# The reciprocal of the attention sums on VectorE alone, in place of two ScalarE steps and a Newton step

## The reference, cut to what matters

```python
x = x + attention(conditioning1(x, fside, fside, w1, u1, cond))      # 16 heads of 32, causal
x = x + ffn(conditioning2(x, fside, fside, w2, u2, cond))            # 512 -> 2048 -> 512, rounded to small floats

# conditioning: a forward and a backward scan over the tokens
ek, ekv = exp(min(k, 30)), exp(min(k, 30)) * v
nf, df = scan(a * decay + ekv), scan(b * decay + ek)                 # and the same in reverse
num, den = nf + nb - ekv + euk * v, df + db - ek + euk
out = sigmoid(r) * num / max(den, 1e-8) * (0.8 + 0.2 * tf)

# attention
scores = where(causal, q @ k.T / sqrt(32), -inf)
probs = softmax(scores)                                              # exp(s - max) / sum
attn = probs @ v
return attn @ w_o.T
```

## Time and profile before

| | us |
|---|---|
| median of 3 runs | 918.21 |
| lowest and highest of them | 915.83, 919.13 |
| the profiled execution, its time | 914.99 |
| the profiled execution, its span | 913.2 |
| mean granted TensorE clock | 0.934 |

### The profile page before, as it was taken

One profiled execution on the slowest core, in us unless ns is written; L12 is line 12 of the kernel. 1 busy time (PEld: TensorE's weight loads), 2 busy tenths in 40 slices (PEclk: granted clock), 3 DMA queues, 4 the chain that ended last, 5 costly groups with the idle time before them and its releaser, 6 DMA issues.

```text
span 913.2 us, 10845 instructions
## 1 busy us (share of the span) xinstructions
PE 759.0 (83%) x3985; PEld 391.3 (43%) x3985; DVE 772.7 (85%) x1122; ACT 471.0 (52%) x710; POOL 73.8 (8%) x149
## 2 busy tenths in 40 slices
PE   4666649298889899897998999978989998999595
PEld 1222224144444344454543444544434445554483
DVE  4999999999997879889988799799887896543887
ACT  4965655358575361476653623766545325453350
POOL 1000001011100002111000021110000120200000
PEclk9676769699999999999899999999999999999798
DMA  9622211256300003754000037540000084500001
GB/s 337 256 76 90 104 57 47 57 126 163 81 23 13 1 12 93 196 150 116 13 24 1 11 73 216 151 104 24 17 7 13 15 207 113 128 1 1 1 1 46
DMA packets 30820, 72.27 MB, mean 79 GB/s; under 512 B 5808, under 2 KB 6832, under 8 KB 28976
## 3 DMA queue, kind: packets, MB, share of 16 engines
q1 hardware_dynamic: 19584, 46.67, 17.1%
q0 software_dynamic: 6144, 16.79, 7.8%
q10 hardware_dynamic: 5040, 8.14, 2.7%
HBM read 33.82 MB, written 4.19 MB: 42 GB/s over the span
## 4 chain that ended last, share of the span: by engine, by line
PE 42%; DVE 34%; issue 8%; ACT 6%; DMA 6%; SPq 3%; POOL 1%; ACTq 0%; DVEq 0%
PE bank L1499 9%; DMA stacks<-rows 5%; PE bank L1394 5%; PE bank L1306 5%; PE bank L1511 5%; PE bank L1365 3%; PE bank L1383 3%; DVE negmax L1029 3%; SPq L318 3%; PE bank L1410 2%; PE bank L1367 2%; PE bank L1332 2%; ACT region L530 2%; DVE fn L909 2%; PE bank L1298 2%
## 5 line engine op out<-in xcount | busy, mean ns | idle before, releaser
L1029 DVE TENSOR_REDUCE negmax<-bank 128x4 f32<-128x512 f32 (+2 forms) x96 | 98.7, 1035 | 39.1 <-PE bank L1339 20.6
L1365 PE MATMUL bank<-stacks 128*128 128x512 f32 (+3 forms) x256 | 106.0, 420 | 28.9 <-ACT region L530 21.0
L530 ACT ACTIVATE region<-bank 128x384 f32<-128x384 f32 (+1 forms) x192 | 95.7, 524 | 63.1 <-PE bank L1368 60.4
L318 POOL DMA_DIRECT2D stacks<-rows x128 | 69.8, 553 | 721.0 <-DVE region L806 350.2
L1306 PE MATMUL bank<-h,wqkv 128*128 128x512 f32 x256 | 115.2, 601 | 4.2 <-DVE region L1259 4.2
L1332 PE MATMUL bank<-stacks 128*128 128x128 f32 (+3 forms) x256 | 79.8, 406 | 7.2 <-DMA stacks<-rows 4.8
L1367 PE MATMUL bank<-maxrow,pick 128*128 128x512 bf16 (+3 forms) x256 | 82.9, 324 | 0.0
L1365 PEld LDWEIGHTS bank<-stacks 128*128 128x128 f32 x256 | 51.8, 202 | 59.0 <-ACT region L530 38.5
L1306 PEld LDWEIGHTS bank<-h,wqkv 128*128 128x128 f32 x256 | 48.4, 193 | 61.5 <-issue 55.4
L1298 PE MATMUL bank<-wqkv,h 128*128 128x512 f32 x128 | 60.9, 620 | 4.7 <-DVE h L957 4.7
L1552 PE MATMUL bank<-region,ident 128*128 128x512 f32 x64 | 49.0, 926 | 11.9 <-DVE identb L860 11.9
(11 more groups left out here) (178 smaller groups left out, 1485.6 us busy)
## 6 DMA issues: line engine op xcount, KB each, us to landing
stacks<-rows SPq DMA_DIRECT2D x128, 128.0 KB, 4.1
stacks<-rows POOLq DMA_DIRECT2D x128, 128.0 KB, 4.7
kt<-in_fside ACTq DMA_DIRECT2D x30, 256.0 KB, 3.3
region<-in_w_gate SPq DMA_DIRECT2D x4, 1024.0 KB, 11.3
h<-in_x SPq DMA_DIRECT2D x4, 1024.0 KB, 5.6
xt<-in_x SPq DMA_DIRECT2D x4, 1024.0 KB, 7.8
region<-in_w_up SPq DMA_DIRECT2D x4, 1024.0 KB, 6.2
region<-in_w_down SPq DMA_DIRECT2D x4, 1024.0 KB, 4.7
```

The lines of the kernel that those rows point to most:

```text
L318: eng.dma_start(stacks[HD * r:HD * r + HD, at:at + 2, i, :].bitcast(F32), rows[mine, q:k + 1:k - q, :]).then_inc(stacked[s][i], 16)
L530: nc.scalar.activation(probs[:, i, P_AT[tiles[0]]:P_AT[tiles[0]] + columns], bank[4 + n % 2][:, 0:columns], ACT.Exp, scale=SCALE).then_inc ...
L1029: nc.vector.tensor_reduce(o, scored, AX_X, ALU.max, negate=True).then_inc(max_taken, 1)
L1365: nc.tensor.matmul(o, ks[s][:, i, P * t:P * t + P], qs[s][:, i, P * t:T], start=True, stop=False, skip_group_check=True)
```

## The change

The two ScalarE steps and their semaphore go. VectorE waits for `pv_ready` itself, takes the reciprocal of bank 7 with its own instruction and multiplies bank 6 with it. Both versions have 16 divisions, four to a turn; the place of each on VectorE stays as it was, and no other instruction changes places.

```diff
-        newton, divided, rsum_ready, refined = sem("newton"), sem("divided"), sem("rsum_ready"), sem("refined")
+        newton, divided, refined = sem("newton"), sem("divided"), sem("refined")
...
-            def sum_reciprocal(b, g):
-                act.wait_ge(pv_ready, b * GROUPS + g + 1)
-                nc.scalar.activation(rsum[:, :], bank[7][:, :], ACT.Ln).then_inc(rsum_ready, 1)
-                act.wait_ge(rsum_ready, b * (2 * GROUPS) + 2 * g + 1)
-                nc.scalar.activation(rsum[:, :], rsum[:, :], ACT.Exp, scale=-1.0).then_inc(rsum_ready, 1)
-
...
-                sum_reciprocal(b, 0)
...
-                sum_reciprocal(b, 1)
...
-                sum_reciprocal(b, 2)
...
-                sum_reciprocal(b, 3)
...
             def normalise(b, g):
 
                 G = b * GROUPS + g
-                dve.wait_ge(rsum_ready, b * (2 * GROUPS) + 2 * g + 2)
-                nc.vector.tensor_tensor(attn[g], bank[7][:, :], rsum[:, :], ALU.mult).then_inc(refined, 1)
-                dve.wait_ge(refined, 2 * G + 1)
-                nc.vector.scalar_tensor_tensor(rsum[:, :], attn[g], 2.0, rsum[:, :], ALU.subtract, ALU.mult).then_inc(refined, 1)
-                dve.wait_ge(refined, 2 * G + 2)
-                nc.vector.scalar_tensor_tensor(attn[g], bank[6][:, :], -1.0, rsum[:, :], ALU.mult, ALU.mult).then_inc(normed, 1)
+                dve.wait_ge(pv_ready, G + 1)
+                nc.vector.reciprocal(rsum[:, :], bank[7][:, :]).then_inc(refined, 1)
+                dve.wait_ge(refined, G + 1)
+                nc.vector.tensor_tensor(attn[g], bank[6][:, :], rsum[:, :], ALU.mult).then_inc(normed, 1)
```

## The result

The changed kernel takes 933.41 us, median of 4 runs (932.64 to 934.9), against 917.42 for the kernel before, median of 4 (915.83 to 919.13). The ratio is 1.0176, with a 95% interval of 1.0152 to 1.020: 16.1 us slower, 13.9 to 18.3. The profiled execution took 932.64 us.

What follows compares the result with a forecast made beforehand. VectorE was taken to bound the stretch from 221 to 261 us. Turns 0 to 2 at 3.8 + 1.5 = 5.3 us each make 16.0, turn 3 adds 0: +16 on the 918.21 median, 934 us, range 922 to 950.

Steps and rivals of the forecast that it cites:

- What bounds the kernel: Turns 0 to 2, 221 to 261 us in batch 0: VectorE is busy 39.32 of 40 us and has no room.
- The size of R: Duration of VectorE's reciprocal over 512 columns, taken as 3.3 us, with 1.3 and 3.9 kept as ends.
- the reading from the long steps: Reciprocal's duration with a fixed part of 149 ns, leaving 29 ns for four columns, 7.3 a column: 3.9 us.
- Groups 0 and 1: Their divisions in turns 0 to 2: nothing absorbs 2 x 1.9 us, so group 3's transposed maxima come 3.8 us later.
- Group 2 hidden: Group 2's division, turns 0 to 2: 1.9 us more on VectorE fits in the 3.05 or 2.5 us of room.
- ScalarE's relief: TensorE's wait for group 3's exponentials goes with ScalarE's two steps in group 2: about 0.5 us a turn.
- Groups 2 and 3: Up to the second residual sum, turns 0 to 2: TensorE 1.3 us late, VectorE 1.5; the larger counts, 1.5 a turn.
- Turn 3: Batch 3, where VectorE has room: maxima may hold TensorE's scores about 0.5 us, group 2 gives 0.5 back; sum 0.
- The profile after: VectorE's busy time grows by 31 us; TensorE shows a new wait of about 1.3 us for `rows` in turns 0 to 2.

Runs made afterwards that it cites:

- the run on groups 0 and 1: Only the divisions of groups 0 and 1 in turns 0 to 2 use VectorE's reciprocal, against the kernel before: 930.34 us, ratio 1.0141.
- the runs with one of the two groups: Two kernels: only group 2, or only group 3, in turns 0 to 2 uses VectorE's reciprocal, against the kernel before: 916.32 and 916.90 us.

## Why the prediction was right

The forecast was 934.0 us, and +16; measured were 933.41 and +16.1. By its own steps:

- **What bounds the kernel.** The stretch on VectorE in turns 0 to 2, from 221 to 261 us, absorbs nothing. Shown by the run on groups 0 and 1 (+12.9; 3.77 us in each turn of the trace) and, with the sign turned, by the stretch without the Newton step (-2.8, -2.1 and -2.6 us).
- **The size of R.** 3.3 us was taken, 3.35 measured. I took a fixed part of 159 ns and divided the other 19 by three steps between four columns, which gives 6.3 ns a step and 3.4 us, and took a little less. The measured line is the same: 153 ns + 6.25 a column is 159 ns + 6.25 for each step from the first column to the last, and the durations can't tell the two forms apart. That I had the fixed part to within a ns was luck. Each ns of it moves R by 0.17 us, and the 159 came from a slip: the neighbour at 161 less its own three steps at 1.04 ns is 158, which gives 3.6, and less its four columns it is 157, which with four columns gives 2.8. In the reading from the long steps (149 ns fixed, four columns, 3.9 us) the 4 ns that the fixed part is too small are worth 0.5 us at 512 columns. One row of four columns could not decide between 2.6 and 3.9, and the range said so.
- **Groups 0 and 1**, forecast 3.8 us a turn. In batch 0 the transposed maxima of group 3 are 3.8 late. The timed run gives 4.3 a turn, with 3.5 to 5.0, and the traces 3.76 in each turn.
- **Group 2 hidden, ScalarE's relief.** The values of group 3 start at 275.97, 54.59 us after VectorE's row at 221.38, against 51.16 before: 3.4 later, 3.8 less 0.34 of relief. The forecast for the relief was 0.5; in turn 3 it is 0.50.
- **Groups 2 and 3**, forecast 1.5 us a turn, as the larger of TensorE's lateness (1.3) and VectorE's (1.5). TensorE waited 1.44 us in batch 0, VectorE's waits of 0.82, 0.57 and 0.87 are gone, the timed run gives 4.5 for three turns, and the traces 1.38 in each. VectorE's lateness is the one that counts: in turn 1 TensorE waited only 0.43 us, since it came to the projection 1.0 us later, and the stretch was as long as in the others (27.24). That it is the excess over the waits, and not a price per division, is shown by the runs with one of the two groups, whose traces have no added time.
- **Turn 3**, forecast 0: timed 1.000. The two sides that the forecast weighed, 0.5 us for the maxima of group 3 and 0.5 back from ScalarE, are both in the traces, as 0.6 later and 0.5 back.
- **The profile after.** VectorE's busy time grew by 30.2 us, forecast 31. The waits of L1382 for `rows` in turns 0 to 2 are 1.44, 0.43 and 1.44 us, forecast 1.3 each.

The duration in this trace is 3.35 us, and 6.25 ns a column is six times the 1.04 of an ordinary column. The rule of the Trainium skill that spoke against the change (the page "VectorE: DVE Perf Modes", "First, the fixed hardware budget": an iterated divide with a repeat count of 8), read as eight cycles a column, would have given an estimate of 4.4 us and +31. It pointed the right way; in size the measurement decides, and it doesn't agree.

In the profiled executions alone the difference is 17.65 us, a little more than in the medians. The two stretches of turns 0 to 2 make 15.4 of it, the change's own work. 1.7 is the feed-forward part of turn 1, at a lower granted clock; the rest is small differences of both signs outside the two stretches.

## What to carry to other kernels

An instruction that replaces four isn't cheaper for being one: with 3.35 us the reciprocal is 4.9 ordinary steps over the same 512 columns. A logarithm and an exponential on an engine with room and a Newton step (2.05 us of VectorE for the whole division, against 3.99) beat it in this kernel where VectorE is full, and where VectorE waits it is nearly free. Cost a moved step place by place: the same 1.94 us cost 1.9 us each in the full stretch, nothing alone in front of waits of 2.3 us, and 1.4 us for two together there. Where the timed runs are too coarse to tell, compare the same stretch in the traces, turn by turn. When a short instance is the only row of an operation, read it with the fixed part of its neighbours, keep all the readings, and let the range carry them.

## What was not expected of the hardware

The reciprocal takes 153 ns + 6.25 ns a column from 4 to 512 columns of float32 in SBUF. At 512 columns it takes as long from PSUM (3347 against 3353 ns) and with a bfloat16 result, or source and result, in SBUF (3353 each).

The place where TensorE's clock falls decides what that costs. In the kernel without the Newton step the granted clock is 0.83 over the first 10 us of the feed-forward part and 1.00 in the next 10: that is a third of those 10 us at 1.2 GHz and the rest at 2.4, while TensorE was busy for 9.82 us of the 10. The part then takes 1.7 us more. The profile after has the same in one turn of three, with 61.12 us against 59.44:

```profile
507.45:568.57 61.12, 59.62 (x234) 26.45 (x234) 50.04 (x65) 24.78 (x29) 4.87 (x8) 0.97 0.18 44
```

The kernel before has it in none of its turns 0 to 2, and the eight other profiles have it in 13 of their 24. With that goes that the profiled execution before lies 2.4 us under its median, and the one after 0.8 under.

In the stretch that VectorE bounds a lower clock cost nothing. With all divisions changed it took the same 43.26 us at 0.93, 0.84 and 0.88:

```profile
221.38:264.64 43.26, 33.12 (x242) 18.89 (x241) 42.67 (x51) 24.09 (x44) 4.23 (x8) 0.93 0.27 68
414.88:458.13 43.25, 33.86 (x229) 19.51 (x231) 42.66 (x50) 23.59 (x44) 4.43 (x8) 0.84 0.27 68
610.11:653.37 43.26, 34.55 (x241) 19.95 (x240) 42.67 (x50) 24.05 (x44) 4.21 (x8) 0.88 0.26 67
```

So two profiled executions can differ by several us with the same work, and a difference of that size is read from timed runs, or from stretches that the clock doesn't touch. Ahead of the feed-forward part TensorE waits 2.3 us for VectorE in turns 0 to 2, before and after, where the clock falls then as where it doesn't. Why it falls in some executions and turns and not in others stays open.
